# Post-norm decoder layer with a top-2 mixture of experts on one core: batch 14's second output projection moves to another PSUM bank and ahead on TensorE, the first tile table moves ahead on VectorE, and two waits leave the row of scatters on GpSimd

## The chip, the cores and the metric

One core of a Trainium2 chip runs the whole program in one launch. The metric is the device time in microseconds (us), as the median of several executions. Lower is better. Engines are written as the profile writes them: PE is TensorE's matmuls, PEld its weight loads, DVE is VectorE, ACT is ScalarE, POOL is GpSimd, and SPq is the DMA queue that the sync engine (SP) issues to.

## The reference

The input is 16 batches of 128 tokens with 256 features (`x`) and a context of the same shape. Three sublayers follow each other, each with a residual sum and a layer norm behind it:

```
x = layernorm(x + linear_attention(x))       # softmax(q) over features, softmax(k) over tokens, k^T v, norm, Wo
x = layernorm(x + cross_attention(x, ctx))   # 16 heads of 16, softmax over 128 context tokens, Wo
x = layernorm(x + moe(x))                    # 8 experts, hidden 512, exact gelu, top 2 of a softmax gate

def moe(xt):                                 # 2048 tokens
    g = gelu(xt @ wg1 + bg1); probs = softmax(g @ wg2)
    top_vals, top_idx = top_k(probs, 2)      # gates: the two probabilities, zero elsewhere
    h = gelu(einsum('nd,edh->enh', xt, w_in)); o = einsum('enh,ehd->end', h, w_out)
    return einsum('ne,end->nd', gates, o)
```

The kernel computes each token's two experts only: it sorts tokens by expert and works on tiles of one expert's tokens.

## The kernel before

**Attention part.** Sixteen batches run through a software pipeline. Each engine has its own list of steps (`step:batch`), written out by hand: a head, a repeated middle and a tail. The tails are what the change edits. Engines meet through counting semaphores only, and each executes its list in order. The steps that matter here, with the lines of the kernel, are these.

- PE `mT` turns the row maxima of the scores into PSUM bank 5 (`B_MT`, L1591); ACT `MTc` copies them (L654) and counts `s_mT`.
- PE `sc` makes the scores of one batch in banks 2, 1, 4 and 3 (L1609 and L1613, 32-row tiles) and counts `s_sc`, 4 per batch. ACT `ex0` to `ex3` (L739) exponentiate one bank each and count `s_ex`.
- PE `pv` (L1630, L1634) forms weighted values and row sums in bank 7 and counts `s_pv`, 4 per batch. ACT `lns` and `rec` (L743, L748) turn the sums into reciprocals.
- DVE `O2T` and `nr` (L1173, L1193, L1195) scale the values and count `s_o2T`.
- PE `ao2` (L1647, through the helper line L1324) is the second output projection, four matmul records. It writes bank 1 (`B_AO2`), which is also the bank of `ex1`; so `ao2:b` waits until the next batch's `ex1` has read it (`through(s_ex, 4, 2, b + 1)`).
- DVE `R2` adds the residual, `s2` takes statistics, POOL `pw2` raises them to the power -1/2 (L521), and DVE `n2` (L1205) writes the normed row into the record `REC`. PE `x2T` transposes it (L1329), ACT copies it, and `gh`, `gcp`, `gelu` and `lg` make the gate's logits.

**Routing.** Batches fall into three groups, 0 to 9, 10 to 13, and 14 and 15. For each group `g`, DVE `choice1:g` and `choice2:g` find the two best experts (L905 to L916), PE `cnt:g` counts how many earlier tokens chose each (L1366, L1358), DVE `gate1`, `dest`, `gate2` (L921 to L944) make gates and row numbers, and POOL then issues one indirect DMA for each batch and choice: `sc:0` to `sc:19` scatter group 0 to the buckets in HBM, `sc:20` to `sc:27` group 1, `sc:28` to `sc:31` group 2 (all L536; a POOL step `sc:n` is a scatter, a PE step `sc:b` a score). In POOL's tail stand steps that only wait: `past_sc:14` waits until PE's `sc:14` is counted, `past_pv:15` until `pv:15` is, and so on.

**Tile tables.** DVE `full:0` to `full:3` work out from group 0's counts which expert tiles 0 to 2 belong to and where their rows start: `full:1` five small instructions, `full:2` seven (ending with L989, which counts `s_tables`), `full:3` three. Each is followed by a wait for its own end.

**Expert part.** SP waits for `s_pv` of all batches, for `s_tables` and for all group 0 scatters, then loads tiles 0, 1 and 2 (L408). Tiles 3 and on wait for a second table and for all scatters. PE transposes a tile (`turn`, L1387), ACT and DVE split it into a high and a low half (`high`, `low`, L654 and L1063), PE multiplies it by w_in (`up`; its first half is `upa`, L333), ACT applies gelu twice (L805), DVE forms the low half (L1241), PE multiplies by w_out (`down`, L1428). The two results of each token are scattered to `parts` in HBM and summed at the end.

PE's tail order around the change is:

```
sc:14 nat:15 ao2:13 pv:14 mT:15 sc:15 x2T:12 ao2:14 x2T:13 pv:15 cntpre:1 gh:13 ao2:15 lg:1
x2T:14 x2T:15 gh:15 cnt:1 cntpre:2 lg:2 turn:0 upa:0 cnt:2 turn:1 upb:0
```

ACT's tail there is `ex0:15 X2T:12 ex1:15 ex2:15 ex3:15 X2T:13 lns:15 rec:15`.

Of the kernel before, what the change touches and what calls it, by code (L numbers as in the profile page):

```python
# [30 lines left out]
ALU = mybir.AluOpType  # L31
AX = mybir.AxisListType

NB, S, D = 16, 128, 256
# [29 lines left out]
FO, FQ2, FO2, NFL = 0, 256, 512, 768  # L64
# [7 lines left out]
def decoder_layer(nc, x, ctx, wpack, rows, vecs, wg1, bg1, wg2, w_in, w_out, out):  # L72
# [3 lines left out]
    with es:  # L76
# [25 lines left out]
        wf = weights[:, KC * NHL:KC * (NHL + NFL)].rearrange("p (k n) -> p k n", k=KC)  # L102
# [28 lines left out]
        R1, R2 = ([r[:, k, :] for r in R] for k in range(2))  # L131
# [15 lines left out]
        O2T = [t[:, 0, :, :] for t in NT]  # L147
# [8 lines left out]
        XR = [scratch[:, EARLY * P + D * k:EARLY * P + D * (k + 1)] for k in range(3)] + [sb("XR3", [P, D])[:]]  # L156
# [314 lines left out]
        def _(pool):  # L471
# [67 lines left out]
            def emit(step, b, p, half):  # L539
# [59 lines left out]
                if step == "past_mT":  # L599
# [8 lines left out]

            def put(t):
# [221 lines left out]
        def _(dve):  # L831
# [244 lines left out]
            def emit(step, b, p, half):  # L1076
# [100 lines left out]
                if step == "R2":  # L1177
                    dve.wait_ge(s_ao2, b + 1)
                    dve.wait_ge(s_x1b, b + 1)
                    if past(b, 2):  # L1180
                        dve.wait_ge(s_x2, b - 1)
                    dve.tensor_tensor(R2[p], bank[B_AO2][:, 0:D], XR[b % 4], ALU.add).then_inc(s_r2, 1)
                if step == "ewl" and b >= 1:
                    e, q = (b - 1) // 2, (b - 1) % 2
                    dve.wait_ge(s_ewh, b)
# [32 lines left out]
                if step == "whose":  # L1218
# [12 lines left out]

            def hidden_low(t):
# [71 lines left out]
        def _(pe):  # L1304
# [16 lines left out]
            def full(dst, a, b):  # L1321

                for c in range(KC):
                    last = pe.matmul(dst, a(c), b(c), start=(c == 0), stop=(c == KC - 1))  # L1324
                return last
# [6 lines left out]
            def through(signal, each, part, at):  # L1332

                if isinstance(at, int):
                    at = min(at, NB - 1)
                    if at < 0:
                        return
                pe.wait_ge(signal, each * at + part)
# [98 lines left out]
            def emit(step, b, p, half):  # L1437
# [199 lines left out]
                                last.then_inc(s_pv, 1)  # L1637
                if step == "ao2":
                    pe.wait_ge(s_o2T, b + 1)
                    through(s_ex, 4, 2, b + 1)  # L1640
                    if counted:
                        through(s_r2, 1, 1, b - 1)
                        through(s_st, 2, 2, b + 3)
                    full(bank[B_AO2][:, 0:D], lambda c: O2T[p][:, c, :], lambda c: wf[:, c, FO2:FO2 + D]).then_inc(s_ao2, 1)
                if step == "x2T":
                    pe.wait_ge(s_x2, b + 1)
                    through(s_qkT, 1, 1, b + 5)  # L1647
# [39 lines left out]
                if step == "cntpre":  # L1687
# [3 lines left out]
                         "kv2/1", emit,  # L1691
# [4 lines left out]

            e, e_next = held[0], expert_of(1)
# [52 lines left out]
```

## Time and profile before

| | us |
|---|---|
| median of 3 executions | 423.39 |
| lowest and highest | 420.61, 423.83 |
| the profiled execution's own time | 426.17 |
| its span, first to last instruction | 424.4 |

The profiled execution's time is its span of 424.4 us and 1.77 us around it. The span has three parts: attention with a steady pipeline until about 230 us, a transition until about 280 us in which the last batches, the gate and the sorting chain end and the first expert tiles begin, and the expert tiles with the final sum. In a timeline, each row is a start, a length, an engine, a line, an operation with its output and input and the number of instructions merged, and in brackets the idle time before it with what ended that. A releaser called "remote" means that a semaphore arrived and no instruction's recorded end stands beside it; "issue" means that nothing visible was waited for.

### The profile page before, as it was taken

To read this page: it belongs to the slowest core of one execution; us is meant where nothing else is said; L and a number is where in the kernel's file an instruction comes from. 1 tells how busy PE (TensorE), PEld (TensorE's weight loads), DVE (VectorE), ACT (ScalarE), POOL (GpSimd) and SP (SyncE) were. 2 spreads that over 40 slices of the span, in tenths; PEclk is the share of its full clock that TensorE was granted. 3 is DMA by queue.
4 is the path that set the end of the run, shared out by engine and by line. 5 is a ranking of instruction groups with operands and counts; after the bars stand their busy time and mean duration, and the time that the engine had idled before them with its cause. 6 is when DMAs were issued, how large, how long until landed. Compare 5 with 4: busy or idle time off the path is not lost. (4 is left out here: it accounts for less than half of the span.)

```text
span 424.4 us, 12165 instructions
## 1 busy us (share of the span) xinstructions
PE 342.2 (81%) x4025; PEld 278.2 (66%) x4025; DVE 308.1 (73%) x913; ACT 221.5 (52%) x518; POOL 219.5 (52%) x287
## 2 busy tenths in 40 slices
PE   2977999999999999999887475767999999998100
PEld 1655777877778777787666343556899999987100
DVE  3767989888988888888877717368777756666193
ACT  3436676666666667667855334262544444443044
POOL 8335456675657757576447761733133332423273
PEclk9999999999999999999899965599999999999755
DMA  7610222220222102221011220515525277594493
GB/s 233 174 72 1 78 76 76 76 75 6 76 76 79 54 24 76 79 76 51 2 52 68 76 91 26 166 65 163 170 68 157 83 256 267 193 343 178 134 373 124
DMA packets 22683, 47.86 MB, mean 113 GB/s; under 512 B 3840, under 2 KB 11264, under 8 KB 21472
## 3 DMA queue, kind: packets, MB, share of 16 engines
q1 hardware_dynamic: 18064, 35.54, 25.6%
q0 software_dynamic: 3408, 9.44, 6.1%
q10 hardware_dynamic: 1152, 2.10, 1.3%
q8 instruction: 36, 0.59, 0.6%
q14 instruction: 23, 0.19, 0.1%
HBM read 24.75 MB, written 12.89 MB: 89 GB/s over the span
## 5 line engine op out<-in xcount | busy, mean ns | idle before, releaser
L615 POOL DMA_INDIRECT parts<-QKT,rows_all x39 | 38.4, 984 | 75.6 <-DVE QKT L1249 68.3
L521 POOL TENSOR_TENSOR rstd<-veps,neghalf 128x1 f32<-128x1 f32 x48 | 38.7, 807 | 39.4 <-DVE veps L886 39.1
L333 PE MATMUL bank<-QS,EW 128*128 128x256 f16 x240 | 43.6, 279 | 4.3 <-DVE XB L1063 2.8
L1241 DVE TENSOR_TENSOR R<-scratch,QV 128x512 f16<-128x512 f32 x39 | 26.8, 691 | 25.9 <-ACT scratch L805 14.7
L805 ACT ACTIVATE scratch<-bank 128x512 f32<-128x512 f32 x39 | 23.4, 600 | 38.3 <-PE bank L333 28.9
L536 POOL DMA_INDIRECT bkt<-REC,dest x32 | 32.3, 1008 | 19.2 <-issue 8.0
L1167 DVE TENSOR_REDUCE NM<-bank 128x4 bf16<-128x512 f32 x64 | 39.6, 679 | 2.2 <-PE bank L1579 1.9
L739 ACT ACTIVATE rows_all<-bank 128x512 f32<-128x512 f32 x64 | 33.2, 603 | 12.0 <-PE bank L1613 6.8
L1428 PE MATMUL bank<-EW,QV 128*128 x240 | 36.1, 273 | 2.0 <-DVE R L1241 1.2
L333 PE MATMUL bank<-XCTh,weights 128*128 128x128 f16 x256 | 28.1, 225 | 7.6 <-ACT rows_all L739 7.6
L333 PE MATMUL bank<-XB,EW 128*128 128x256 f16 x120 | 33.5, 279 | 0.0
L333 PE MATMUL bank<-weights,XCTh 128*128 128x512 f16 (+1 forms) x128 | 31.8, 338 | 2.0 <-DVE XCTl L1080 2.0
L333 PEld LDWEIGHTS bank<-QS,EW 128*128 x240 | 24.1, 100 | 8.0 <-issue 4.9
L654 ACT ACTIVATE QS<-bank 128x512 f16<-128x512 f32 (+1 forms) x24 | 12.5, 520 | 32.0 <-PE bank L1387 32.0
L333 PEld LDWEIGHTS bank<-XCTh,weights 128*128 128x128 f16 x256 | 21.5, 101 | 10.4 <-ACT rows_all L739 9.7
L1428 PEld LDWEIGHTS bank<-EW,QV 128*128 128x128 f16 x240 | 22.9, 98 | 6.3 <-issue 3.6
L550 POOL TENSOR_TENSOR QE<-QE,qrec 128x256 f32<-128x256 f32 x16 | 10.0, 622 | 29.6 <-DVE qrec L1124 29.6
L1324 PE MATMUL bank<-weights,NT 128*128 128x256 f32 x64 | 19.0, 424 | 6.9 <-issue 3.5
L333 PE MATMUL bank<-XCTl,weights 128*128 128x128 f16 x128 | 24.2, 225 | 0.0
L805 ACT ACTIVATE QV<-bank 128x512 f16<-128x512 f32 x39 | 23.4, 601 | 0.0
L1428 PE MATMUL bank<-EW,R 128*128 x120 | 22.9, 273 | 0.0
L1249 DVE SCALAR_TENSOR_TENSOR QKT<-bank,rows_all 128x256 f32<-128x256 f32 x39 | 17.5, 480 | 6.5 <-DMA parts<-QKT,rows_all 4.9
(264 smaller groups left out, 1010.3 us busy)
## 6 DMA issues: line engine op xcount, KB each, us to landing
scratch<-w_in SPq DMA_DIRECT2D x8, 512.0 KB, 3.5
scratch<-w_out SPq DMA_DIRECT2D x8, 512.0 KB, 3.4
weights<-EW SPq DMA_DIRECT2D x4, 1024.0 KB
rows_all<-bkt SPq DMA_DIRECT2D x15, 264.0 KB
REC<-EW SPq DMA_DIRECT2D x3, 1024.0 KB
XC<-x SPq DMA_DIRECT2D x16, 128.0 KB, 3.3
XC<-ctx SPq DMA_DIRECT2D x16, 128.0 KB, 3.3
scratch<-EW SPq DMA_DIRECT2D x2, 1024.0 KB
```

The source lines that it names most:

```text
L333: last = pe.matmul(dst, a(c), b(c), start=(c == 0 and i == 0), stop=(c == n - 1 and i == 2))
L521: pool.tensor_tensor(rstd[n][p][:], veps[n][p][:], neghalf[:, 0:1], ALU.pow).then_inc(s_rs[n], 1)
L536: pool.indirect_dma_start(bkt, bass.IndirectOffsetOnAxis(ap=dest[:, k, b:b + 1], axis=0), REC[:, b, :], None)\
L615: pool.indirect_dma_start(parts, bass.IndirectOffsetOnAxis(ap=home[:, t, f:f + 1], axis=0), Y[t % 2][:, f, :], None).then_inc(s_put[t % 2] ...
L654: act.activation(dst, src, ACT.Copy, scale=scale).then_inc(signal, 1)
L739: act.activation(EX[p][:, u, :, :], chunks(bank[SC_BANK[u]], 4), ACT.Exp, scale=DH ** -0.5)\
L805: act.activation(dst[t % 2][:, hc * g:hc * g + hc, 0:n * P], chunks(bank[2 * (t % 2) + g], hc, n * P), ACT.Gelu, scale=2.0 / WSCALE).then_ ...
L1167: dve.tensor_reduce(NM[p][:, u, 0:4], chunks(bank[NAT_BANK[u]], 4), AX.X, ALU.max, negate=True).then_inc(s_mx, 1)
L1241: dve.tensor_tensor(HL[t % 2][:, part, 0:n * P], HF[t % 2][:, part, 0:n * P], HH[t % 2][:, part, 0:n * P], ALU.subtract).then_inc(s_hl, 1)
L1249: dve.scalar_tensor_tensor(Y[t % 2][:, f, :], bank[4 + t % 2][:, f * D:(f + 1) * D], gate[:, t, 0, f:f + 1], TX[t % NX][:, f, 0:D], ALU.mu ...
L1324: last = pe.matmul(dst, a(c), b(c), start=(c == 0), stop=(c == KC - 1))
L1428: last = pe.matmul(bank[4 + t % 2][:, f * D:(f + 1) * D], a[t % 2][:, h, f * P:(f + 1) * P], b[:, h, :], start=(h == 0 and i == 0 and f == 0),
```

## The change

Three edits in the tails, nothing else.

1. **PE and DVE, batch 14's `ao2`.** For batch 14 alone the output goes to bank 5 (`B_MT`) instead of bank 1. The wait for the next batch's `ex1` is replaced by one for `s_mT` of all 16 batches, and `R2:14` reads bank 5. In PE's order `ao2:14` moves one place forward, ahead of `x2T:12`.
2. **DVE's order.** `full:1`, `full:2` and `full:3` move ahead of batch 15's sums: `full:1` from behind `nr:15`, `full:2` from behind `choice2:1`, `full:3` from behind `gate2:1`, all to a place between `s2:14` and `O2T:15`. `n2:14` moves there too, from behind `s2:15`.
3. **POOL's order.** The steps `past_sc:15` and `past_pv:15` go. `pw2:14` moves from behind `sc:15` to behind `sc:13`, and `pw2:15` from ahead of `sc:19` to behind it.

```diff
 POOL
-"sc:11 past_mT:15 sc:12 sc:13 past_sc:15 sc:14 sc:15 pw2:14 sc:16 sc:17 past_pv:15 sc:18 pw2:15 sc:19 "
+"sc:11 past_mT:15 sc:12 sc:13 pw2:14 sc:14 sc:15 sc:16 sc:17 sc:18 sc:19 pw2:15 "
 DVE
-    dve.tensor_tensor(R2[p], bank[B_AO2][:, 0:D], XR[b % 4], ALU.add).then_inc(s_r2, 1)
+    dve.tensor_tensor(R2[p], bank[B_MT if b == 14 else B_AO2][:, 0:D], XR[b % 4], ALU.add).then_inc(s_r2, 1)
-"mx3:15 R2:13 s2:13 ewl:15 O2T:14 nr:14 n2:13 ewl:16 R2:14 s2:14 O2T:15 nr:15 full:1 R2:15 s2:15 n2:14 "
-"choice1:1 n2:15 choice2:1 full:2 gate1:1 dest:1 gate2:1 full:3 "
+"mx3:15 R2:13 s2:13 ewl:15 O2T:14 nr:14 n2:13 ewl:16 R2:14 s2:14 full:1 full:2 n2:14 full:3 O2T:15 nr:15 R2:15 s2:15 "
+"choice1:1 n2:15 choice2:1 gate1:1 dest:1 gate2:1 "
 PE
     pe.wait_ge(s_o2T, b + 1)
-    through(s_ex, 4, 2, b + 1)
+    if b == 14:
+        pe.wait_ge(s_mT, NB)
+    else:
+        through(s_ex, 4, 2, b + 1)
...
-    full(bank[B_AO2][:, 0:D], lambda c: O2T[p][:, c, :], lambda c: wf[:, c, FO2:FO2 + D]).then_inc(s_ao2, 1)
+    full(bank[B_MT if b == 14 else B_AO2][:, 0:D], lambda c: O2T[p][:, c, :], lambda c: wf[:, c, FO2:FO2 + D]).then_inc(s_ao2, 1)
-"... mT:15 sc:15 x2T:12 ao2:14 x2T:13 pv:15 "
+"... mT:15 sc:15 ao2:14 x2T:12 x2T:13 pv:15 "
```

## Rows read from the trace of the kernel before

**Rows 1.** The page's first line, and two stretches: busy time, count, clock, DMA.
```profile
span 424.4 us, 12165 instructions
...
240.00:250.00 10.00, 6.48 (x68) 4.47 (x64) 4.05 (x9) 2.83 (x7) 7.97 (x9) 0.69 0.27 95
...
330.00:370.00 40.00, 40.00 (x393) 36.41 (x391) 25.32 (x73) 18.12 (x36) 14.38 (x15) 1.00 0.58 201
```

**Rows 2.** Timeline of PE from 218 to 282 us.
```profile
220.90 1.09 PE L1613 MATMUL bank<-QM,K 32*128 32x256 f32 x16
...
239.67 1.09 PE L1613 MATMUL bank<-QM,K 32*128 32x256 f32 x16
...
244.64 2.04 PE L1324 MATMUL bank<-weights,NT 128*128 128x256 f32 x4 [3.52 <-issue]
...
247.05 1.94 PE L1630 MATMUL bank<-rows_all,V 128*32 128x128 f32 x32
248.75 2.05 PE L1634 MATMUL bank<-rows_all,onesq 128*32 128x256 f32 x16
...
255.43 2.08 PE L1324 MATMUL bank<-weights,NT 128*128 128x256 f32 x4 [2.20 <-DVE NT L1195]
...
263.44 0.25 PE L1358 MATMUL bank<-selh,ones 128*128 128x32 f16 x4
...
267.45 1.11 PE L1387 MATMUL bank<-ident,rows_all 128*128 128x128 f32 x4 [1.29 <-DMA rows_all<-bkt]
...
272.67 0.19 PE L1358 MATMUL bank<-selh,ones 128*128 128x16 f16 x2
```

**Rows 3.** Timeline of ACT from 218 to 290 us.
```profile
222.14 2.06 ACT L739 ACTIVATE rows_all<-bank 128x512 f32<-128x512 f32 x4 [0.48 <-PE bank L1613]
...
243.18 0.60 ACT L739 ACTIVATE rows_all<-bank 128x512 f32<-128x512 f32 x1 [3.08 <-remote]
...
243.94 1.58 ACT L739 ACTIVATE rows_all<-bank 128x512 f32<-128x512 f32 x3
...
253.04 0.38 ACT L743 ACTIVATE LS<-bank 128x256 f32<-128x256 f32 x1 [5.50 <-remote]
```

**Rows 4.** Timeline of DVE from 218 to 282 us.
```profile
241.19 0.43 DVE L1195 TENSOR_TENSOR NT<-NT 128x256 f32<-128x256 f32 x1
...
241.85 1.22 DVE L1186 SCALAR_TENSOR_TENSOR EW<-scratch,EW 128x1024 f16<-128x1024 f32 x1
...
253.90 0.69 DVE L1173 TENSOR_TENSOR NT<-bank,RS 128x512 f32<-128x512 f32 x1 [5.81 <-ACT RS L748]
...
258.89 0.41 DVE L1205 TENSOR_SCALAR REC<-R,mv,rstd 128x256 f32<-128x256 f32 x1
...
263.32 0.17 DVE L989 TENSOR_SCALAR base<-base_f 128x3 int32<-128x3 f32 x1
...
264.03 0.19 DVE L940 TENSOR_TENSOR at_row<-bank,ecap 128x32 f32<-128x32 f32 x1
...
276.63 0.17 DVE L940 TENSOR_TENSOR at_row<-bank,ecap 128x16 f32<-128x16 f32 x1 [4.26 <-remote]
```

**Rows 5.** Timeline of POOL from 218 to 290 us.
```profile
242.09 1.82 POOL L536 DMA_INDIRECT bkt<-REC,dest  x1 [0.30 <-issue]
...
253.81 0.96 POOL L536 DMA_INDIRECT bkt<-REC,dest  x1 [1.76 <-remote]
259.05 0.69 POOL L521 TENSOR_TENSOR rstd<-veps,neghalf 128x1 f32<-128x1 f32 x1 [4.28 <-DVE veps L886]
259.93 1.04 POOL L536 DMA_INDIRECT bkt<-REC,dest  x1 [0.19 <-issue]
265.82 0.96 POOL L536 DMA_INDIRECT bkt<-REC,dest  x1 [4.86 <-DVE REC L928]
...
274.68 0.96 POOL L536 DMA_INDIRECT bkt<-REC,dest  x1 [0.30 <-issue]
```

**Rows 6.** Timeline of SP's DMA queue from 218 to 290 us.
```profile
264.66 25.16 SPq L408 DMA_DIRECT2D rows_all<-bkt  x4
```

2 rows, old and new, of the table start are left out of this document.

## The prediction

> **What bounds the kernel now.** I read the busy time by stretch first. From 330 to 370 us PE is busy for all of 40.00 us, so a delay or a gain carried into the expert tiles stays in the end time. In the stretch 240 to 250 us PE is busy 6.48 of 10 us at a granted clock of 0.69 of full, POOL 7.97 us, DVE and ACT 4.05 and 2.83: nothing is full, the transition is one chain of waits [rows 1]. The chain view covers only the final sum, so I put the chain together from the timelines of the engines.
>
> It runs as follows. PE's `sc:15` ends by its record at 239.67 + 1.09 = 240.76, but ACT's `ex0:15` starts only at 243.18, released by "remote"; `ex1` to `ex3` of batch 15 end at 243.94 + 1.58 = 245.52 [rows 2, 3]. PE's `ao2:14` starts at 244.64, when `ex1:15` has emptied bank 1, after 3.52 us of idle PE, and takes 2.04. Only then does `pv:15` run, from 247.05 to 248.75 + 2.05 = 250.80 by the records [rows 2]. ACT's `lns:15` starts at 253.04, again "remote", DVE's `O2T:15` at 253.90 after 5.81 us idle, PE's `ao2:15` at 255.43 [rows 2 to 4]. From there a chain of small steps (statistics, power, norm, transpose, gate) leads through `lg:2`, which ends where the idle time before `turn:0` begins, at 267.45 - 1.29 = 266.16 [rows 2].
>
> Beside it runs a second branch: `cnt:1` ends at 263.44 + 0.25 = 263.69, `dest:1` starts at 264.03, and that opens the row of eight scatters from 265.82 to 274.68 + 0.96 = 275.64 [rows 2, 4, 5]. `cnt:2` ends by its record at 272.67 + 0.19 = 272.86, yet `dest:2`, which waits for it, starts at 276.63 after 4.26 us idle [rows 2, 4]. `low:1`, `up` of tile 1, the last four scatters and the table of tile 3 are behind `dest:2` in order.
>
> **The odd thing in these rows** is the lateness of PE's signals: 243.18 - 240.76 = 2.42 us for `sc:15`, 253.04 - 250.80 = 2.24 for `pv:15`, 276.63 - 272.86 = 3.77 for `cnt:2`, where the same signal of `sc:13`, with no scatter under way, was 222.14 - 220.90 - 1.09 = 0.15 late [rows 2 to 4]. All three stand beside POOL's scatters. Two of them arrive soon after a scatter that had no successor: the row of eight ended at 275.64, 0.99 before 276.63; the scatter ahead of the one at 253.81 ended at 253.81 - 1.76 = 252.05, 0.99 before 253.04 [rows 3 to 5]. The third, `sc:15` at 243.18, arrived in the middle of a row, while the scatter of 242.09 was being held for 1.82 us [rows 3, 5].
>
> **The change part by part.**
>
> *`ao2:14`.* Its operand is ready at 241.19 + 0.43 = 241.62 and bank 5 is free by then, as `sc:15` needed the turned maxima before 239.67 [rows 2, 4]. It now runs in the 3.52 us in which PE idled. It costs between 1.0 us (half of 2.04, at full clock) and 2.04, so it ends between 242.7 and 243.7. `x2T:12` is now behind it: two of the four transposes of `turn:0`, 0.55 us by half of 1.11, hence 243.2 to 244.2 [rows 2]. ACT's copy of it stands between `ex0:15` (ends 243.78) and `ex1:15`, so the exponentials are late by 0 to 0.4 us; I take 0.1. `pv:15` then starts when `ex3:15` ends, at 245.6 instead of 247.05: a gain of 1.4 us, with 1.0 and 1.53 as bounds [rows 2, 3].
>
> *`pv:15`'s own length and lateness.* It took 3.75 us from start to recorded end at the half clock and its signal 2.24 more [rows 2, 3]. I keep both, as nothing in the edit shortens them by itself. Bounds: at the full clock it would be 1.9 long; the signal can be 0.15 late as for `sc:13`, or wait for the end of the row of scatters. The latter is now later: without `past_pv:15`, two more scatters follow the end at 252.05 at 0.96 + 0.30 each, so the row ends at 254.57, and 0.99 later is 255.56 [rows 5].
>
> *The tables.* `full:1`, `full:2`, `full:3` are 15 instructions of the kind of L989, 0.17 long and about 0.21 apart, 3.2 us. They move into DVE's idle 5.81 us ahead of `O2T:15` and are hidden [rows 4]; with 1.4 us less idle there 4.4 are left, still enough. If `pv:15` came over 4 us earlier the cover would be just gone. `s_tables` comes about 11 us before 263.49. SP's loads, at 264.66 now, then wait for scatter 19 alone. That one ends at 254.57; it was issued at 259.93 and the loads began 4.73 later without waiting for more than the table, so 254.6 + 4.7 = 259.3 is a safe bound for them [rows 4 to 6]. `turn:0` no longer waits for data and follows `lg:2`: 1.29 us gained there [rows 2].
>
> *DVE's queue behind it.* `n2:14` (0.41) leaves the place ahead of `choice1:1`, so `n2:15`, and with it `x2T:15`, `gh:15` and `cnt:1`, come 0.33 earlier (0.41 less the overlap of neighbours). `full:2` leaves the place ahead of `dest:1`, which started 264.03 - 263.69 = 0.34 after `cnt:1`; that goes too. Together 0.65, between 0.3 and 0.7 [rows 2, 4].
>
> *POOL.* `pw2:14` moves ahead of two scatters and is ready in time. `pw2:15` now stands behind scatter 19, which ends at 254.57, while its input came at 259.05 before and would come at 257.6: no cost [rows 5].
>
> *Here a rule bears on the sum.* The scatter at 242.09 took 1.82 instead of 0.96 us, beside DVE's L1186 from 241.85 to 243.07 [rows 4, 5]. The Trainium skill (SBUF — State Buffer, section "SBUF: two separate sides") says that GpSimd and certain DVE instructions, those in a two-port mode or with two SBUF operands, take a shared port pair as an exclusive lock. The trace agrees for this pair of rows. By this rule the 15 table instructions would hold up the scatters that they now run beside, by 3.2 us at the very most, which would cost nothing in my forecast and up to 3.2 more in the slower rival below.
>
> *What of it reaches the end.* The tail is set by `cnt:2`'s signal. I take it as tied to the row of scatters that `dest:1` opens, so it moves with that row: 1.4 + 0.65 = 2.05 us earlier. The 1.29 at `turn:0` then only lengthens the lateness of `cnt:2` and is not counted. Were the signal tied to PE's own work, the gain would be 1.4 + 0.33 + 1.29 = 3.0. Behind it all waits keep their order and PE fills up [rows 1], so 2.1 us come through: 426.17 - 2.1 = 424.1 for a profiled execution, and from the median 423.39 - 2.1 = 421.3. The profiled execution stands 2.8 us above that median.
>
> **The rivals.**
>
> *A, slower: the scatters in a row hold back `pv:15`'s signal until they end.* For it: two of three late signals came 0.99 after a row's end. Against it: `sc:15`'s came in mid-row. It decides if the signal comes at 255.56 instead of 253.04: 2.5 later, 0.65 back, +1.9 us, 425.3. With more of the port lock above, up to 428.5.
>
> *B, much faster: the clock and the signal both come good.* PE now works between 241.6 and 244.2, where it idled before its clock fell. If `pv:15` runs at 2.4 GHz (1.9 us) and its signal is prompt, it is there at 247.6, 5.4 us earlier. `pw2:15` would then wait for scatter 19's end at 254.57 instead of 259.05, which caps the gain near 4.5; with 0.65 that is 5.1: 418.3. Against it: the three late signals. The Trainium skill (TensorE: Matmul & The Clock Gate, section "What's actually happening") says that idleness throttles the array and activity releases it; by this rule B's half with the clock would come true, which alone is worth 1.8 us, and the trace agrees in so far as the 0.69 stands where PE idled.
>
> *C, no change: the gain at `pv:15` is met by a longer lateness.* The signals' lateness grew from 2.2 to 3.8 us with the number of scatters in a row. If it absorbs what is won, 423.4, give or take 0.7.
>
> **How the numbers follow.** My forecast, a gain of 0.8 to 3.6 us (419.8 to 422.6) with 421.3 as its value: 0.38. A: 0.27. B: 0.13. C: 0.22. The range runs from 418.0, which takes in most of B, to 425.6, A's value with its rounding; A with a port lock beyond it and B's extreme are left out, about 0.15 together. The forecast's own range is 419.8 to 422.6. One per cent is 4.2 us, about what a measurement of this kernel can tell from no change: under 419.2 lie B and a sliver of the forecast, 0.15; above 427.6 only A with the port lock, 0.03; between, 0.82.
>
> **What would show it right or wrong.** Right: `ao2:14` starts near 241.7 without waiting for ACT; `pv:15` starts near 245.6 and `lns:15` near 251.6; the base table ends near 252; `turn:0` has no idle time on a DMA; the row of eight scatters starts about 2 us earlier and `dest:2` about 1 us behind its end. Wrong: `lns:15` at 255 or later behind a row of scatters (A); `pv:15` under 2 us long with a prompt signal (B); `dest:2` no earlier than 276.6 though the scatters are (C); or `ex1:15` late because `x2T:12` is.

## The result, and the profile after

| | before | after |
|---|---|---|
| median of 19 executions each | 423.83 | 427.17 |
| lowest and highest | 420.61, 425.15 | 424.09, 431.92 |
| the profiled execution's own time | 426.17 | 426.60 |
| its span | 424.4 | 424.9 |

The changed kernel is slower: 1.0065 of the time before, with a 95% interval of 1.0047 to 1.0084. (The ratio leaves out four of the changed kernel's executions, which lie above 431 us and count as slow, so it is less than the quotient of the medians, 1.0079.) The two profiled executions differ by 0.43 us only. They show what happened, but not the size of the median's loss; a second profile of the changed kernel stands further below (428.45 us).

The first view is PE's timeline of the changed kernel, to be read against [rows 2].

```profile
241.11 1.13 PE L1324 MATMUL bank<-weights,NT 128*128 128x256 f32 x4 [0.94 <-DVE NT L1195]
...
244.94 1.93 PE L1630 MATMUL bank<-rows_all,V 128*32 128x128 f32 x32 [0.76 <-issue]
246.62 1.96 PE L1634 MATMUL bank<-rows_all,onesq 128*32 128x256 f32 x16
...
263.76 1.09 PE L1387 MATMUL bank<-ident,rows_all 128*128 128x128 f32 x4
...
268.96 0.20 PE L1358 MATMUL bank<-selh,ones 128*128 128x16 f16 x2
269.01 1.09 PE L1387 MATMUL bank<-ident,rows_all 128*128 128x128 f32 x4
...
271.43 0.27 PE L333 MATMUL bank<-QS,EW 128*128 128x256 f16 x1
...
276.18 0.28 PE L333 MATMUL bank<-QS,EW 128*128 128x256 f16 x1 [4.04 <-DVE XB L1063]
```

`ao2:14` starts at 241.11 and no longer waits for ACT. `pv:15` starts at 244.94 instead of 247.05, `turn:0` at 263.76 instead of 267.45 and without its idle time on a DMA. `cnt:2` and `turn:1` end by the record at 269.16 and 270.10, and the last matmul of `up:0` (tile 0) at 271.70. Up to here everything is 2 to 4 us earlier. Then PE stands idle.

Next ACT's timeline, in which PE's signals are seen to arrive (its first row answers to the last of [rows 3]).

```profile
249.46 0.38 ACT L743 ACTIVATE LS<-bank 128x256 f32<-128x256 f32 x1 [4.34 <-PE bank L1634]
...
274.72 0.60 ACT L654 ACTIVATE QS<-bank 128x512 f16<-128x512 f32 x1 [7.06 <-remote]
275.33 1.28 ACT L794 ACT_TABLE_LOAD   x1
...
280.42 0.60 ACT L805 ACTIVATE scratch<-bank 128x512 f32<-128x512 f32 x1 [3.81 <-remote]
```

`pv:15`'s signal comes 249.46 - 248.58 = 0.88 us after its recorded end. But `high` of tile 1, which waits for `turn:1`, starts 274.72 - 270.10 = 4.62 late, and the first gelu of tile 0, which waits for `up:0`, 280.42 - 271.70 = 8.72 late. Of these 8.72 us the last 3.81 cost time: until 276.61 ACT was busy with `high` and its table load. The same two operations in the kernel before, from ACT's timeline:

```profile
277.34 0.60 ACT L654 ACTIVATE QS<-bank 128x512 f16<-128x512 f32 x1 [5.94 <-PE bank L1387]
...
279.25 0.60 ACT L805 ACTIVATE scratch<-bank 128x512 f32<-128x512 f32 x1
```

`up:0` had ended there by PE's timeline at 275.27 + 0.27 = 275.54:

```profile
275.27 0.27 PE L333 MATMUL bank<-QS,EW 128*128 128x256 f16 x1
```

So the operation that was 2.62 us early is followed by one that is 1.17 us late. DVE's timeline of the changed kernel shows what happened to `dest:1` and `dest:2` (answering to [rows 4]):

```profile
245.94 0.18 DVE L989 TENSOR_SCALAR base<-base_f 128x3 int32<-128x3 f32 x1
...
261.56 0.19 DVE L940 TENSOR_TENSOR at_row<-bank,ecap 128x32 f32<-128x32 f32 x1 [0.87 <-PE bank L1358]
...
270.51 0.17 DVE L940 TENSOR_TENSOR at_row<-bank,ecap 128x16 f32<-128x16 f32 x1 [1.82 <-PE bank L1358]
```

And POOL's timeline of the changed kernel, the first of the row that `dest:1` opens, its seventh and eighth, the one after it and the last (answering to [rows 5]):

```profile
263.36 1.04 POOL L536 DMA_INDIRECT bkt<-REC,dest  x1 [6.13 <-DVE REC L928]
...
272.29 0.96 POOL L536 DMA_INDIRECT bkt<-REC,dest  x1 [0.30 <-issue]
273.55 0.96 POOL L536 DMA_INDIRECT bkt<-REC,dest  x1 [0.30 <-issue]
...
277.34 0.96 POOL L536 DMA_INDIRECT bkt<-REC,dest  x1 [0.30 <-issue]
```

This is what turned the gain into a loss. `dest:2` runs at 270.51, 6.12 us earlier than before and in the middle of the row of eight, which ends at 272.29 + 0.96 = 273.25. Group 2's four scatters therefore follow with the usual 0.30 us between them, and the row of eight becomes a row of twelve that ends at 278.30. In the kernel before, POOL paused between the two rows, from 275.64 to the next row of its timeline:

```profile
278.61 0.96 POOL L536 DMA_INDIRECT bkt<-REC,dest  x1 [2.97 <-DVE REC L928]
```

In that pause of 2.97 us `cnt:2`'s signal came (276.63) and `turn:1`'s (277.34). `up:0`'s was there by 279.25 at the latest: ACT, busy until then with the table load, started the gelu without idle time. In the changed kernel there is no pause, and `up:0`'s signal comes 2.12 us behind the row of twelve. The busy time by stretch of the changed kernel and then of the kernel before, 270 to 280 and 280 to 290 us, with the granted clock as the third number from the end:

```profile
270.00:280.00 10.00, 5.19 (x35) 3.69 (x34) 2.35 (x12) 1.88 (x2) 6.47 (x7) 0.84 0.31 109
280.00:290.00 10.00, 8.02 (x48) 5.83 (x48) 7.42 (x28) 4.51 (x9) 0.00 (x0) 0.62 0.00 1
```

```profile
270.00:280.00 10.00, 7.12 (x46) 5.64 (x47) 4.39 (x25) 3.55 (x7) 5.51 (x7) 0.77 0.23 84
280.00:290.00 10.00, 9.26 (x84) 7.82 (x82) 7.82 (x29) 5.92 (x12) 2.76 (x3) 1.00 0.16 56
```

PE is busy 5.19 us instead of 7.12 in the first stretch, and in the second it does 48 matmuls at 0.62 of the full clock instead of 84 at full clock. The clock does not fall in the idle time or at its end: the granted clock stands at 1.00 of full (2.4 GHz) from 272 to 277 us, through PE's 4.04 us of idle time, and `up:1` begins at 276.18 in matmuls of 0.27 us. It is 0.70 between 277 and 278 and 0.50 (1.2 GHz) from 278 on, with matmuls of 0.42 us. In the kernel before, PE was idle for 2.81 us at the same place, and the full clock goes on. What was won by 270 us is gone by 290.

### The profile page after: what moved, and what is told of

Read it like the earlier page. It is cut to its first block and busy times, and to the rows that moved or that the text cites. A ratio compares the mean times of both kernels' runs of the same rounds, so it can differ in the third digit from the quotient of the medians.

```text
span 424.9 us, 12161 instructions
## 1 busy us (share of the span) xinstructions
PE 342.6 (81%) x4025; PEld 278.4 (66%) x4025; DVE 308.8 (73%) x913; ACT 221.6 (52%) x518; POOL 219.0 (52%) x287
## 5 line engine op out<-in xcount | busy, mean ns | idle before, releaser
L333 PE MATMUL bank<-QS,EW 128*128 128x256 f16 x240 | 45.0, 284 | 6.6 <-DVE XB L1063 5.5
L1428 PE MATMUL bank<-EW,QV 128*128 x240 | 37.6, 281 | 2.6 <-DVE R L1241 1.7
L333 PE MATMUL bank<-weights,XCTl 128*128 128x512 f16 (+1 forms) x64 | 21.7, 338 | 0.0
```

The source lines that it names most:

```text
L333: last = pe.matmul(dst, a(c), b(c), start=(c == 0 and i == 0), stop=(c == n - 1 and i == 2))
L1428: last = pe.matmul(bank[4 + t % 2][:, f * D:(f + 1) * D], a[t % 2][:, h, f * P:(f + 1) * P], b[:, h, :], start=(h == 0 and i == 0 and f == 0),
```

## The experiments

The theory after the result: POOL's scatters in a row hold back the signals of PE's finished work, and the pause between the row of eight and the row of four is where these were delivered. The change moves `cnt:2` so far ahead that the pause closes. Rivals: the price is the tables' early place on DVE by itself; or the exchange of PE's order; or the long row of group 0's scatters (edit 3).

Each ratio below is against the kernel before, run beside it on the same chip; its medians there were 424.8 or 424.9, where it had 423.8 beside the changed kernel above. So ratios can be compared across the experiments, medians only to about 1 us. One new POOL step is used, `past_up:0`, a wait that lasts until PE has counted `up:0`:

```diff
+                if step == "past_up":
+                    pool.wait_ge(s_up, b + 1)
```

**Edit 1 alone.** The kernel before with `ao2:14` in bank 5 and ahead of `x2T:12`.

```diff
-"... sc:15 x2T:12 ao2:14 x2T:13 pv:15 "
+"... sc:15 ao2:14 x2T:12 x2T:13 pv:15 "
```

> The kernel before with batch 14's second projection moved alone (bank 5, its wait, its place on PE). Theory 'long row': what the change loses is lost where the scatters of groups 1 and 2 merge into one row of twelve, because cnt:2's signal came 6 us earlier. Here turn:0 still waits for its tile loads behind the late base table, so upa:0 and cnt:2 keep their place behind the loads; pv:15 starts about 1.5 us earlier, dest:1 1 to 1.5 us earlier; time 0.5 to 2 us below before (421.8 to 423.3 beside 423.8). Rival 'bank move itself': if the projection's new place delays ex1 to ex3 of batch 15 through ACT's copy of x2T:12, ex3:15 ends after 245.6 and the time is 0 to 1 us above before.

Measured: 424.39 us, ratio 1.0005 (0.9973 to 1.0037). `pv:15` ends by the record at 246.69, 4.11 us earlier than in [rows 2], but its signal comes only 1.01 us earlier, as ACT's timeline of this kernel has it:

```profile
252.03 0.38 ACT L743 ACTIVATE LS<-bank 128x256 f32<-128x256 f32 x1 [7.11 <-remote]
```

It is 5.34 us late, in spite of POOL's `past_pv:15`, which stands in this kernel and waits for the same signal. What PE wins here, the signal's lateness can take.

**Edit 2 alone.** The kernel before with DVE's new order.

> The kernel before with DVE's new order alone (full:1 to full:3 and n2:14 ahead of batch 15's sums). The base table ends near 250 instead of 263.49, but scatter 19 still stands behind pw2:15, issued near 260 and landed near 262.4, so SP's first load moves from 264.66 to about 262.7. Theory 'long row': turn:0 goes from 267.45 to about 266.2, cnt:2 is ready 1.2 us earlier, and the outcome hangs on whether its signal still comes behind the end of the row of eight: if so within 1 us of before; if it comes in mid-row, the rows merge and hidden of tile 0 starts after 279.25, 0 to 3 us above before. Rival 'the lost pause at pv:15': no loss here, since past_pv:15 stands; 0.5 to 1.5 us below before.

Measured: 427.79 us, ratio 1.011 (1.0057 to 1.0164). This edit by itself does damage; that it does more than all three together (1.0065) isn't shown, as the intervals overlap and this one rests on four executions. POOL's timeline of it, the eighth scatter of the row, the ninth and the last:

```profile
275.20 0.96 POOL L536 DMA_INDIRECT bkt<-REC,dest  x1 [0.30 <-issue]
277.70 0.96 POOL L536 DMA_INDIRECT bkt<-REC,dest  x1 [1.54 <-issue]
...
281.49 0.96 POOL L536 DMA_INDIRECT bkt<-REC,dest  x1 [0.30 <-issue]
```

PE's timeline of it, `turn:1` and the end of `up:0`, and ACT's, which waits for the two:

```profile
272.44 0.91 PE L1387 MATMUL bank<-ident,rows_all 128*128 128x128 f32 x4
...
274.39 0.27 PE L333 MATMUL bank<-QS,EW 128*128 128x256 f16 x1
```

```profile
278.55 0.60 ACT L654 ACTIVATE QS<-bank 128x512 f16<-128x512 f32 x1 [7.49 <-remote]
...
282.24 0.60 ACT L805 ACTIVATE scratch<-bank 128x512 f32<-128x512 f32 x1 [1.79 <-remote]
```

The pause has shrunk to 1.54 us. PE's `up:0` ends at 274.66, 0.88 us before it did in the kernel before (275.54 by the record), but its signal is seen at 282.24, 7.58 late, at the end of the last row (282.45).

**Edit 3 alone.** The kernel before with POOL's new order.

> The kernel before with POOL's new order alone (past_sc:15 and past_pv:15 away, pw2:14 and pw2:15 moved). Rival 'the lost pause at pv:15': pv:15 runs as late as before (recorded end near 250.8), now inside a row of scatters that ends near 254.6, so its signal comes up to 2.5 us later than 253.0 and the time is 1 to 3 us above before: all of the loss of the change. Theory 'long row': the loss here is what this signal costs, 0 to 2.5 us, but dest:1, cnt:2 and the row of eight move with it and do not merge; at most half of the loss of the change.

Measured: 425.43 us, ratio 1.0045 (1.0009 to 1.0081), a small loss. In its profiled execution the pause is 2.87 us, the gelu of tile 0 starts at 278.33 and the span is 424.2, so that execution doesn't show where the loss of the median lies. `pv:15`, the signal that loses its pause here, is seen only 0.15 us late in it.

**The changed kernel with a pause ahead of `sc:28`.** The direct test of the theory: nothing that PE or DVE does is changed.

```diff
-"sc:20 sc:21 sc:22 sc:23 sc:24 sc:25 sc:26 sc:27 sc:28 sc:29 sc:30 sc:31"
+"sc:20 sc:21 sc:22 sc:23 sc:24 sc:25 sc:26 sc:27 past_up:0 sc:28 sc:29 sc:30 sc:31"
```

> The changed kernel with one wait more on POOL: ahead of scatter 28 it waits until PE has counted up of tile 0. Theory 'long row': the row of twelve is broken after eight (end near 273.2), so turn:1 is seen near 274 and up of tile 0 near 274.3, hidden of tile 0 starts at about 276 to 277 (after ACT's table load) instead of 280.4, the last four scatters start near 275; time 3 to 5 us below the changed kernel, 1 to 2 below before (421.5 to 423). Rivals 'the lost pause at pv:15' and 'late ao2:15 signal': this wait mends nothing there, it only delays four scatters by 1 to 2 us; time equal to the changed kernel or above, 427 or more.

Measured: 424.84 us, ratio 1.0017 (0.9981 to 1.0053). It can no longer be told from the kernel before, but its interval still touches that of the changed kernel (from 1.0047), and the gain of about 2 us that I expected isn't there. Its profiled execution, a late one of 428.64, shows one cause. PE's timeline, then ACT's:

```profile
248.47 1.94 PE L1632 MATMUL bank<-rows_all,V 128*32 128x128 f32 x32 [1.01 <-issue]
250.16 1.52 PE L1636 MATMUL bank<-rows_all,onesq 128*32 128x256 f32 x16
```

```profile
257.39 0.38 ACT L745 ACTIVATE LS<-bank 128x256 f32<-128x256 f32 x1 [8.74 <-remote]
```

`pv:15` ends at 251.68 and is seen at 257.39, 5.71 late and 1.32 behind the end of group 0's row (256.07). That is the mechanism of rival A of the prediction: the first row holds `pv:15` in some executions.

**The changed kernel with POOL's old order** (edits 1 and 2).

> The changed kernel with POOL's old order back (past_sc:15 and past_pv:15 in, pw2:15 ahead of scatter 19): edits 1 and 2 together. Theory 'signals need a pause': two things are mended or not. pv:15 gets its pause, but scatter 19 waits for pw2:15 again, so tile loads and turn:0 come after it, as in the run of edit 2 alone; cnt:2's signal can still come in mid-row and the last four scatters follow at once, so most of edit 2's loss stays: 425.5 to 428. Rival 'the loss is the missing pause at pv:15': 422 to 423.5, below before.

Measured: 427.18 us, ratio 1.0033 (0.9984 to 1.0081), not to be told from the changed kernel, and by its interval not from the kernel before either. The pause is 0.84 us, the gelu of tile 0 at 282.70. So the rows merge and the gelu is late without edit 3. That edit 3 costs nothing isn't shown: alone it stood at 1.0045.

**Edit 2 alone, with the pause ahead of `sc:28`.**

> Edit 2 alone (426.3 to 427.9 us) with a wait on POOL ahead of scatter 28 until PE has counted up of tile 0. Theory 'signals need a pause': in edit 2 alone the pause between the rows shrank from 2.97 us (before) to 1.5, up of tile 0, recorded done by 275, was seen at 282.2, inside the last row. With the wait it is seen 1 to 2 us behind the end of the row of eight, hidden of tile 0 starts at 278 to 279.5, and the loss of 3 to 4 us is gone or nearly: 423 to 425. Rival 'the early table or its ops on DVE cost by themselves': unchanged, 426.5 or more.

Measured: 424.36 us, ratio 0.9999 (0.9965 to 1.0034), against 1.011 without the wait. The pause is 2.59 us and the gelu of tile 0 starts at 278.78. The two intervals (1.0057 to 1.0164 without the wait) don't touch. The wait takes edit 2's loss away, and with it the table's early place costs nothing that can be measured here, within 0.4%.

**The changed kernel with all scatters of groups 1 and 2 held until `up:0`.** Not meant to be fast: it takes the scatters away from PE's work in question.

```diff
-"sc:20 sc:21 sc:22 ... "
+"past_up:0 sc:20 sc:21 sc:22 ... "
```

> The changed kernel with the twelve scatters of groups 1 and 2 all held on POOL until PE has counted up of tile 0. No scatter is under way while cnt:2, turn:1 and up of tile 0 run. Theory 'scatters make the signals late': all three signals come within 0.2 us of their recorded ends (4.6 and 8.7 us late in the changed kernel), hidden of tile 0 starts near 272 to 273 instead of 280.4, but up of tile 1 and later signals meet the row of twelve, which now runs from about 272 to 287, and tile 3's load waits for it, to about 289: time 423 to 428, no verdict in that. Rival 'PE's signals are late for a reason of its own (dense runs of short matmuls, the clock)': they stay 2 to 8 us late without scatters.

Measured: 428.76 us, ratio 1.0105 (1.0054 to 1.0156). PE's `turn:1`, and ACT behind it:

```profile
270.89 1.09 PE L1389 MATMUL bank<-ident,rows_all 128*128 128x128 f32 x4
```

```profile
272.02 0.60 ACT L656 ACTIVATE QS<-bank 128x512 f16<-128x512 f32 x1 [2.51 <-PE bank L1389]
272.63 1.28 ACT L796 ACT_TABLE_LOAD   x1
...
274.49 0.60 ACT L807 ACTIVATE scratch<-bank 128x512 f32<-128x512 f32 x1 [0.57 <-PE bank L333]
```

With no scatter under way `turn:1` is seen 0.04 us after its recorded end (271.98), against 4.62 in the changed kernel; `cnt:2` is seen 0.11 late and `up:0` 0.04 (274.45 to 274.49), so the gelu of tile 0 starts at 274.49 instead of 280.42. PE's order of work is the same as in the changed kernel, which leaves nothing of the rival of this run. The kernel is slow in all, because the scatters now end at 290.25 and tile 3, which needs them, is first turned at 297.51 instead of 293.33.

**The changed kernel with both pauses**, one ahead of `sc:16` and one ahead of `sc:28`.

```diff
-"... sc:14 sc:15 sc:16 ... sc:27 sc:28 ... "
+"... sc:14 sc:15 past_pv:15 sc:16 ... sc:27 past_up:0 sc:28 ... "
```

> The changed kernel with two waits on POOL: for pv:15 ahead of scatter 16, and for up of tile 0 ahead of scatter 28. Theory 'signals need a pause': lns:15 starts within 1 us of pv:15's recorded end in every execution (0.9 late in one execution of the changed kernel, about 6 in one with the wait at 28 alone), the executions lie closer together, and the median is 1 to 2 us below that of the wait at 28 alone and of before: 422 to 424. Rival: the held scatters cost what the signals win, because tile loads and the row of eight come later: 424.5 to 427.

Measured: **420.64 us, ratio 0.9924 (0.9894 to 0.9954)**, below both kernels with its whole interval, and better than I had expected. Its timeline of POOL shows both pauses, with the last scatter of the row of eight between them:

```profile
251.73 0.95 POOL L536 DMA_INDIRECT bkt<-REC,dest  x1 [2.02 <-PE bank L1636]
...
270.96 0.98 POOL L536 DMA_INDIRECT bkt<-REC,dest  x1 [0.30 <-issue]
274.42 0.95 POOL L536 DMA_INDIRECT bkt<-REC,dest  x1 [2.48 <-remote]
```

ACT's timeline of it:

```profile
273.52 0.60 ACT L656 ACTIVATE QS<-bank 128x512 f16<-128x512 f32 x1 [7.18 <-remote]
...
275.43 0.60 ACT L807 ACTIVATE scratch<-bank 128x512 f32<-128x512 f32 x1
```

`high` of tile 1 comes 1.58 us after the row's end (271.94), inside the pause, and the gelu follows at 275.43, 4.99 earlier than in the changed kernel. Tile 3 is turned at 287.51, 5.82 earlier, and the span is 418.0.

**Only the pause ahead of `sc:16`.**

> The changed kernel with one wait on POOL, for pv:15 ahead of scatter 16, and none ahead of scatter 28. With the changed kernel, the wait at 28 alone (424.8) and both (420.6) it fills a square of four. Theory 'signals need a pause, at both places': pv:15's signal is prompt, but cnt:2 can come in mid-row and the rows of group 1 and 2 merge, so up of tile 0 is seen late: 423 to 426, between. Rival 'only the pause at pv:15 counts': 420 to 421.5, as with both.

Measured: 423.82 us, ratio 0.9975 (0.9955 to 0.9996). With this the changed kernel stands in a square of four. By ratio to the kernel before: neither pause 1.0065, only the late one 1.0017, only the early one 0.9975, both 0.9924. The late one alone is worth about 0.5%, the early one 0.9%, both together 1.4% (2, 4 and 6 us): about the sum, so they look like two prices. The early pause is clear of the noise with and without the late one; the late one is just clear of it beside the early one, and just short of it alone.

**Both pauses, with DVE's old order** (edit 2 undone).

> Both waits and the moved projection, but DVE's old order (full:1 behind nr:15, full:2 behind choice2:1): the early table taken out of the fastest kernel. Theory: the early table is worth something once the signals are prompt, because turn:0 no longer waits 1.3 us for tile loads and dest:1 is not behind seven table instructions: this kernel is 1 to 2.5 us above the one with both waits, 421.5 to 423.5. Rival 'the early table is worth nothing, it only made the rows merge': the same time, 420.6 within 0.7.

Measured: 421.94 us, ratio 0.9932 (0.9906 to 0.9959). Beside 0.9924 the intervals overlap: with the pauses open, what the early tables are worth can't be told from nothing.

**The kernel before with the wait ahead of `sc:28`.**

> The kernel before with the wait for up of tile 0 ahead of scatter 28, nothing else. Before had a pause of 2.97 us there by itself, in which all held signals came, so theory 'signals need a pause' expects little: 0 to 1.5 us below before, by executions in which cnt:2's signal came in mid-row (before spreads from 420.6 to 428). Rival 'the wait itself helps whatever is around it': 3 us below before.

Measured: 424.25 us, ratio 0.9996 (0.9963 to 1.0028). The wait is worth nothing measurable where the pause is there anyway.

**The changed kernel once more**, for a second profile.

> The changed kernel once more, for a second profile: its executions lie between 424 and 432 us. Theory 'signals are held at random inside a row': the same signals come at other times than in the first profile (then 0.9 us late for pv:15, 2.2 for ao2:15, 1.3 for cnt:2, 4.6 for turn:1, 8.7 for up of tile 0), and the end time follows the sum of these along the chain. Rival 'the lateness is fixed by the order of work': the same lateness at the same places within 0.3 us.

Measured: 428.45 us in one execution, span 426.6. PE's timeline, ACT's and POOL's:

```profile
245.92 1.13 PE L1634 MATMUL bank<-rows_all,onesq 128*32 128x256 f32 x16
...
270.63 1.09 PE L1387 MATMUL bank<-ident,rows_all 128*128 128x128 f32 x4
```

```profile
250.38 0.38 ACT L743 ACTIVATE LS<-bank 128x256 f32<-128x256 f32 x1 [5.16 <-remote]
...
277.84 0.60 ACT L654 ACTIVATE QS<-bank 128x512 f16<-128x512 f32 x1 [8.56 <-remote]
...
282.25 0.60 ACT L805 ACTIVATE scratch<-bank 128x512 f32<-128x512 f32 x1 [2.52 <-remote]
```

```profile
275.59 0.96 POOL L536 DMA_INDIRECT bkt<-REC,dest  x1 [0.73 <-issue]
```

Here `pv:15` ran at full clock and ended at 247.05, and its signal is 3.33 late instead of 0.88. The pause is 0.73 us, `turn:1` ends at 271.72 and is seen 6.12 late, and the gelu of tile 0 starts at 282.25, 1.91 behind the end of the last scatter (280.34).

The profiles line up as follows; all times are us. "Into the row" is the recorded end of `cnt:2` less the start of the first of the eight scatters. "`dest:2`" is its start less the end of the eighth scatter, so a minus means that it came in mid-row. The fifth column is the gelu's start less the end of the eighth scatter.

| kernel | `cnt:2` ends, into the row | `dest:2`, behind the row of eight | pause ahead of `sc:28` | gelu of tile 0 | gelu, behind the row of eight | `turn:3` |
|---|---|---|---|---|---|---|
| before | 7.04 | 0.99 | 2.97 | 279.25 | 3.61 | 292.28 |
| edit 1 alone | 6.96 | 1.02 | 2.99 | 278.26 | 3.63 | 291.02 |
| edit 3 alone | 6.99 | 0.90 | 2.87 | 278.33 | 3.51 | 291.12 |
| before, pause at `sc:28` | 7.13 | 0.23 | 2.54 | 280.20 | 3.55 | 292.58 |
| both pauses, DVE's old order | 7.09 | 0.96 | 2.90 | 275.45 | 3.58 | 288.52 |
| edit 2 alone | 6.22 | -0.44 | 1.54 | 282.24 | 6.08 | 294.39 |
| edits 1 and 2 | 6.20 | -1.15 | 0.84 | 282.70 | 7.45 | 294.73 |
| after, second profile | 5.80 | -1.25 | 0.73 | 282.25 | 7.39 | 294.55 |
| after | 5.80 | -2.74 | 0.30 | 280.42 | 7.17 | 293.33 |
| after, pause at `sc:16` | 5.80 | -1.25 | 0.73 | 278.73 | 7.40 | 290.68 |
| after, pause at `sc:28` | 5.80 | -2.02 | 2.36 | 282.85 | 3.38 | 295.52 |
| edit 2, pause at `sc:28` | 6.28 | -1.14 | 2.59 | 278.78 | 3.60 | 291.17 |
| after, both pauses | 5.80 | -1.23 | 2.48 | 275.43 | 3.49 | 287.51 |

The first two columns show what edit 2 does. In the five kernels with DVE's old order `turn:0` waits 1.2 to 1.4 us for its tile, `cnt:2` ends about 7 us into the row, and `dest:2` comes behind the row's end. In the eight profiles with the new order `turn:0` waits 0 to 0.3 us, `cnt:2` ends 5.8 to 6.3 us into the row, and every time `dest:2` comes in mid-row. Then the last four scatters follow at once, unless a wait holds them.

Where the pause is 2.36 us or more, the gelu starts 3.4 to 3.6 us behind the row of eight; where it is 1.54 us or less, 6.1 to 7.5 us behind it. `turn:3` follows the gelu by 12.0 to 13.1 us in all 13 profiles, so this delay is carried on into the expert tiles. In the three kernels with the new order and the wait at `sc:28`, and in the kernel before with it, this has to be read with care: `past_up:0` lets the row of four go only when `up:0` is counted, so the length of the pause is no choice there, it is how long the signal takes. POOL started its scatter 2.36 to 2.59 us behind the row's end in the three, though PE's record has the work done before that end (at 270.21 with both pauses, against 271.94). Some of it is POOL's own: in the kernel that holds all twelve it starts at 275.27, 0.82 us after `up:0`'s recorded end of 274.45, with no scatter under way. That leaves 1.5 to 1.8 us behind the row's end for the signal. The four profiles whose gelu comes behind the last scatter agree with it, at 1.86 to 2.12 us. (In "after, pause at `sc:28`" everything before had been late already, as told above.)

Not every signal in a row is late, and not every engine's. ACT's timeline of the changed kernel has two more rows that show it: `gcp:13`, which waits for PE's `gh:13`, and `high` of tile 0, which waits for `turn:0`:

```profile
253.80 0.28 ACT L654 ACTIVATE scratch<-bank 128x128 f32<-128x128 f32 x1 [3.51 <-remote]
...
264.89 0.60 ACT L654 ACTIVATE QS<-bank 128x512 f16<-128x512 f32 x1 [1.63 <-PE bank L1387]
```

DVE's timeline and then PE's, in the row of scatters from 246.66 to 254.14:

```profile
251.44 0.43 DVE L1195 TENSOR_TENSOR NT<-NT 128x256 f32<-128x256 f32 x1
```

```profile
248.96 1.12 PE L1667 MATMUL bank<-X2T,wg_f 128*64 128x128 f32 x8
251.92 1.13 PE L1324 MATMUL bank<-weights,NT 128*128 128x256 f32 x4 [1.84 <-issue]
```

`high` of tile 0 (264.89) comes 0.04 us after `turn:0`'s recorded end (264.85), 1.5 us into the very row in which `turn:1`'s signal is then 4.62 late. So it is in all 13 profiles of the table: `turn:0` ends 1.5 to 2.8 us into its row and is seen 0.03 or 0.04 late, `cnt:2` ends 5.8 to 7.1 us into it and is seen 1.35 to 3.87 late. And while `gh:13`'s signal is on its way (ended at 250.08, seen at 253.80, 3.72 late, by an ACT that is idle), DVE's signal at 251.87 starts PE's `ao2:15` at 251.92, 0.05 late in the same row. What comes late here is what PE sends. In a row that follows a long pause, as the rows of eight do (over 4 us without a scatter), it is not late at the start; behind a short one it can be: `pv:15` in the second profile of the changed kernel ended 0.4 us into a row that had followed the one before after 0.79 us, and was 3.33 late.

## Why the prediction was wrong

The forecast was a gain of 2.1 us, to 421.3; the measured median is 427.17, outside the range of 418.0 to 425.6. Step by step:

- **`ao2:14` in PE's idle time, `pv:15`'s start**: right. 241.11 for 241.7, 244.94 for 245.6. The gain at `pv:15` is 2.11 us where 1.4 was forecast, but 0.59 of it stands already at `sc:15` (239.08 for 239.67), ahead of anything that the edits move; without that it is 1.52, inside the bounds of 1.0 to 1.53.
- **`pv:15`'s length and lateness kept at 3.75 and 2.24**: length right (3.64) in one execution and 2.0 in the second, where it ran at the full clock. The lateness was mis-sized as one number. It was 0.88 and 3.33 in the changed kernel, 5.34 with edit 1 alone, 5.71 with the late pause: it differs between executions and is a term with a range of its own, from 0.15 (edit 3 alone) to beyond the row's end. The clock half of rival B came true in one of two executions: in both `ao2:14` ran at the full clock (1.13 us instead of 2.04) with the same work around it, then `pv:15` took 3.64 us in the one and 2.00 in the other. The Trainium skill (TensorE: Matmul & The Clock Gate, section "What's actually happening") has it that idleness throttles and activity releases. The traces agree with it at `ao2:14` and in the 0.62 behind PE's idle time after 272 us; which of the two clocks `pv:15` gets, no run here explains.
- **The tables**: hidden, as said. The base table's last instruction ends at 246.12, ahead of `O2T:15`, and 6 us before the 252 that was forecast. `turn:0` has no wait on its load. That moves it by 3.69 us, more than the chain's gain alone.
- **The port lock**: the 15 small instructions on DVE did not stretch the scatters. The one at 241.53 took 1.82 us beside L1186 again, the others ran beside the tables at 1.16 and 0.96. So its 3.2 us bound stayed unused, and the measured 427.17 lies between rival A's 425.3 and its 428.5 by chance: the lock that was to bring the time up there did not.
- **`dest:1`** came 2.47 us earlier, where 2.05 was forecast. The number is right, in part by luck: `lns:15` came at 249.46 instead of 251.6, 2.1 us earlier than forecast, and then `ao2:15`'s signal, 2.17 us late in the changed kernel and 0.09 in the kernel before, took about as much back. That signal had no term in the sum.
- **"I take it as tied to the row of scatters that `dest:1` opens, so it moves with that row … Behind it all waits keep their order"**: this is the step that failed. [Rows 3] already showed a signal, `sc:15`'s, that came in mid-row, and the prediction said so. `cnt:2`'s did the same here, 1.35 us after its recorded end, and `dest:2` was 6.12 us earlier. The failure is then one step further on: I asked only what an early `dest:2` would win (3.0 us in all, if the signal followed PE). `dest:2` releases four more scatters, and those close the pause of 2.97 us in which the signals of `turn:1` and `up:0` came through. An earlier release on POOL, which was not on the path, triggered the collision.
- **`turn:0`'s 1.29 "then only lengthens the lateness of `cnt:2`"**: wrong for the same reason. It moved `cnt:2` from 7.04 to 5.80 us into the row, and in each of the eight profiles with DVE's new order that was early enough to be seen before the row's end. Edit 2 alone shows the price: 1.011, and 0.9999 with the wait.
- **Rival A** had the mechanism right, scatters in a row that hold PE's signals until they end, but at `pv:15` and group 0's row alone. That place is real too: the pause ahead of `sc:16` takes the changed kernel from 1.0065 to 0.9975, and edit 3 alone costs 1.0045. The second place had no price in the prediction, and what closes it, edit 2, costs 1.011 alone, the largest of the three by its value.
- **Rival C** (what is won is met by lateness) describes edit 1 alone: 4.11 us earlier by PE's record, 1.01 by the signal, nothing in the median.

My expectations of the experiments missed in several places: edit 1 alone gained nothing, edit 2 alone lost as much as I had allowed at most by its median (3.0 us) and more by its ratio, the late pause alone took the loss away but brought no gain, both pauses together came out 1.4 us under the range that I gave, and holding all twelve scatters 0.8 us over it.

What is shown: that the loss comes with the closed pause (edit 2 with and without the wait; both pauses against the early one alone), and that PE's recorded ends can be trusted, since ACT sees them 0.04 us late when no scatter runs. What is open: what in the row holds the signals, POOL's issuing or the transfers behind it; why some come through in mid-row (`cnt:2` 1.35 late, `sc:15` 2.42) and others not; and how short a pause may be. 1.54 us was too short, but the 2.36 to 2.59 us of the runs with `past_up:0` are what the signal took, not a length that was tried. Edits 1 and 3 together without edit 2 were not run, so the shares of the three edits don't add up to the whole with certainty. It also stays open how much of the 3.3 us each late signal makes up, since the two profiled executions of before and after are only 0.43 apart.

## What to carry to other kernels

Before an edit makes a releaser of queued DMA issues earlier, look at the gaps that it closes on that engine, and at which other engines' signals arrived in these gaps: here a pause that looked idle was worth 0.5 to 1.1% of the time, 2 to 5 us. Where matmul ends and the start of their reader differ by microseconds and the releaser is "remote", compare both with POOL's indirect DMAs; a wait in their row, placed where a critical signal is due, can be cheaper than issuing them early.

## What the runs showed of the hardware

- **PE's signals are late beside indirect DMAs in a row.** 0.04 us without scatters (the kernel that holds them), 0.15 for `sc:13` in the kernel before; but up to 8.7 late beside a row in the changed kernel, and 9.5 for `up:0` with the pause at `sc:16` alone (269.25 to 278.73). Early in a row they are prompt: `turn:0`'s 0.03 to 0.04 late, up to 2.8 us into it. The Trainium skill (SBUF — State Buffer, section "SBUF: two separate sides") says that on the engines' side only the port pair shared by GpSimd and DVE causes contention, and that PE and ACT never wait on anyone. The trace agrees as to the work itself where it can be compared: the four matmuls of `turn:1` take 1.09 us at the same clock with a scatter beside them and without one. It says nothing of the signals, which are what comes late here, from PE to ACT, DVE and POOL; DVE's signal to PE in the same row was 0.05 late.
- **Held signals come through behind a row.** With pauses of 2.36 us or more between two rows `turn:1`'s signal was seen 1.5 to 1.7 us behind the first; with 1.54, 0.84, 0.73 and 0.30, `up:0`'s was seen 0.2 us ahead of the second row's end or 1.9 to 2.1 behind it.
- **The clock fell behind the idle stretch, not in it.** In the changed kernel it stood at 1.00 through 4.04 us of idle PE and for about another us of work, and was 0.50 from 278 us on. Between 280 and 290 us it was 0.62 of full, where the kernel before, with 2.81 us idle, had 1.00, and the stretch held 48 matmuls instead of 84.
